# A twelve-stage decoder kernel: reordered rounded feed-forward, weight sums made a stage earlier, constant products in TensorE's waits

## What is computed

```python
def bit_linear(x, w, b):
    gamma_x = clip(max(abs(x), axis=-1, keepdims=True), 1e-05)
    x_int = clip(round(x * 127.0 / gamma_x), -128.0, 127.0)
    gamma_w = clip(mean(abs(w)), 1e-05)
    w_int = clip(round(w / gamma_w), -1.0, 1.0)
    return einsum('bsd,hd->bsh', x_int * gamma_x / 127.0, w_int * gamma_w) + b
# in the block:
h = silu(bit_linear(x, gate_w, gate_b)) * bit_linear(x, val_w, val_b)
out = bit_linear(h, out_w, out_b)
```

## Time and profile before

| | |
|---|---|
| three runs, median (lowest to highest) | 2133.7 us (2133.47 to 2135.55) |
| the profiled execution | 2131.74 us, its span 2130.0 us |
| TensorE, VectorE, ScalarE, GpSimd busy | 85%, 62%, 45%, 24% of the span |
| L0f, from the first norm instruction to that of L1a | 273.3 to 379.2 us |
| mean granted TensorE clock | 0.92 |

### The profile page before, as it was taken

How to read it: one execution, slowest core, us unless ns; L and a number is a source line. 1 busy time by engine, 2 the same in 40 slices (tenths; PEclk the granted TensorE clock), 3 DMA queues, 4 the chain that set the end, 5 groups by cost and what they waited for, 6 DMA issues and landing times. The chain is left out here.

```text
span 2130.0 us, 39122 instructions
## 1 busy us (share of the span) xinstructions
PE 1811.5 (85%) x14754; PEld 1472.3 (69%) x14758; DVE 1316.1 (62%) x2421; ACT 961.3 (45%) x1934; POOL 509.8 (24%) x557
## 2 busy tenths in 40 slices
PE   6877745689999789999757777799999998899798
PEld 4756622468999678888425665577778776788666
DVE  4575577456565654444476765788888886676632
ACT  2343445335555422222214324466667664455532
POOL 1020010023333433532030012344555552000100
PEclk9989966789999899999877987999999999999999
DMA  2020000020000101000100000000010012111000
GB/s 91 3 82 3 3 26 0 15 75 23 26 26 22 67 31 60 30 30 0 39 12 1 3 24 15 23 24 29 30 30 30 30 30 88 40 36 36 2 1 20
DMA packets 13501, 61.47 MB, mean 29 GB/s; under 512 B 1872, under 2 KB 2000, under 8 KB 11216
## 3 DMA queue, kind: packets, MB, share of 16 engines
q1 hardware_dynamic: 13392, 59.95, 8.2%
HBM read 58.90 MB, written 1.05 MB: 28 GB/s over the span
## 5 line engine op out<-in xcount | busy, mean ns | idle before, releaser
L2348 DVE SCALAR_TENSOR_TENSOR arena<-bank,arena 128x508 f32<-128x508 f32 (+2 forms) x204 | 151.7, 744 | 35.0 <-ACT arena L2344 23.0
L2473 PE MATMUL bank<-L3a_wo,L3a_y_gated 128*128 128x256 f32 x512 | 124.1, 387 | 0.0
L2679 DVE TENSOR_TENSOR L3a_decays<-L3a_decays,L3a_cb_masked 128x512 f32<-128x512 f32 x128 | 94.7, 802 | 43.8 <-ACT L3a_decays L2564 43.8
L2496 PE MATMUL bank<-L3a_xnT_high,L3a_w_high 128*128 128x512 f32 x256 | 106.4, 416 | 10.8 <-POOL L3a_w_low L2799 9.2
L2564 ACT ACTIVATE L3a_decays<-bank 128x512 f32<-128x512 f32 x128 | 66.1, 604 | 99.2 <-PE bank L2447 99.2
L1804 PE MATMUL bank<-L1f_xnT_high,L1f_high 128*128 128x512 f32 x256 | 101.6, 397 | 7.6 <-DVE L1f_hidden L1867 7.6
L2473 PEld LDWEIGHTS bank<-L3a_wo,L3a_y_gated 128*128 128x128 f32 x512 | 92.4, 190 | 17.7 <-issue 7.3
L218 PE MATMUL bank<-const,xn 128*128 128x128 f32 x192 | 47.3, 418 | 66.4 <-ACT xn L202 61.0
L1804 PE MATMUL bank<-L1f_xnT_low,L1f_high 128*128 128x512 f32 x256 | 101.2, 395 | 0.0
L1804 PE MATMUL bank<-L1f_xnT_high,L1f_low 128*128 128x512 f32 x256 | 101.0, 394 | 0.0
L1838 ACT ACTIVATE L1f_silu<-bank 128x512 f32<-128x512 f32 x64 | 38.3, 598 | 138.3 <-PE bank L1804 138.3
(11 more groups left out here) (571 smaller groups left out, 5298.8 us busy)
## 6 DMA issues: line engine op xcount, KB each, us to landing
arena<-in_L3p SPq DMA_DIRECT2D x32, 388.0 KB, 3.0
arena<-in_L1f SPq DMA_DIRECT2D x8, 1536.0 KB, 6.7
arena<-in_L1x SPq DMA_DIRECT2D x18, 384.0 KB, 3.0
arena<-in_L3x SPq DMA_DIRECT2D x18, 384.0 KB, 3.0
arena<-in_L0f SPq DMA_DIRECT2D x1, 4224.0 KB, 13.2
arena<-in_L3f SPq DMA_DIRECT2D x1, 4055.0 KB, 12.5
arena<-in_L2x SPq DMA_DIRECT2D x1, 1989.0 KB, 7.9
arena<-in_L0a SPq DMA_DIRECT2D x1, 1571.0 KB, 9.3
```

The lines of the kernel that those rows point to most:

```text
L2348: return nc.vector.scalar_tensor_tensor(dst[:, :, d:], psum[:, :, 0:P - d], wcol, dst[:, :, d:], ALU.mult, ALU.add)
L2473: mm = nc.tensor.matmul(ps[g // 2][:, (g % 2) * C:(g % 2 + 1) * C], yg[:, o, g * P:(g + 1) * P], wo[:, o, :], start=False, stop=False, ski ...
L2496: mm = nc.tensor.matmul(bank(name, half)[:, :], wm[a][:, kc, :], (xh, xl)[b][:, kc, half * HALF:(half + 1) * HALF], start=(kc + at == 0), ...
L2679: nc.vector.tensor_tensor(d, d, cbm[:, 4 * half:4 * half + 4, :].rearrange("p b t -> p (b t)"), ALU.mult).then_inc(S["dec_ready"], 1)
```

## The change

In L0f:
- The sums of absolute weights are taken in L0x, by ScalarE after its last copy: three activations with Abs and an accumulator, written to a buffer that nobody reads. The sums lie in a buffer that outlives the stage.
- The norm makes xn but no transposes and no copies. GpSimd adds the bias after x_int is ready.
- ScalarE takes the first two matrices through both steps before it rounds the third; VectorE's clip of the third comes after x_int and its copy; half of the transposed x_int is copied by ScalarE. ternary(2) comes after silu(0), and silu's table is loaded ahead.
- The loop is written out. Gates and values have separate semaphores. TensorE's order in turn n is gates(n+3), transposes of h(n), values(n+3), projection of n; three gate and three value groups stand ahead of the loop. VectorE's order is gates(n+1), addition to x of n-2, values(n+1), then the product and scales of n. ScalarE's is silu(n+1), copy of h(n-1), two roundings of h(n). g has three buffers; the scales have one column per batch.

In the norm of all other stages TensorE multiplies constants (the identity by the first columns of the constants, fp32) into bank 7: two products 512 wide at the head, and one 256 wide ahead of each wait for batches 1, 2, 3 and 5, 6, 7. In L1f six more, 512 wide, into bank 6 follow the router's products.

```diff
+    def idle(self, pe, n, width=HALF, bank=7):
+        for _ in range(n):
+            self.nc.tensor.matmul(self.k.ps[bank][:, 0:width], self.k.ident, self.k.const[:, 0:width], start=True,
+                                  stop=True)
     def tensor(self, pe):
+        self.idle(pe, 2)
         for h in range(2):
             for j in range(4):
+                if j:
+                    self.idle(pe, 1, C)
                 pe.wait_ge(self.s_xn[by_dve], (self.BY_DVE if by_dve else self.BY_ACT).index(b) + 1)
...
# l0_xattn, ScalarE
                 a.act(act)
+                act.wait_ge(k.after.s_img, 16)
+                for m in range(3):
+                    nc.scalar.activation(a.km[:, m, :, :].rearrange("p c t -> p (c t)"),
+                                         k.after.img[:, m * KC * TOK:(m + 1) * KC * TOK], ACT.Abs,
+                                         accum_out=k.wsum[:, m:m + 1])
...
# l0_ffn, TensorE
-                ln.tensor(pe)
-                pe.wait_ge(s_wsum, 3)
-                nc.tensor.matmul(ps[7][:, 0:3], k.c["ones"], wsum[:, :], start=True, stop=True).then_inc(s_tot, 1)
+                nc.tensor.matmul(ps[7][:, 0:3], k.c["ones"], k.wsum[:, :], start=True, stop=True).then_inc(s_tot, 1)
...
+                for n in range(3):
+                    gates(n)
+                    values(n)
+                for n in range(NB):
+                    s = n % 2
+                    gates(n + 3)
+                    pe.wait_ge(s_hi, n + 1)
+                    since(pe, s_hTc, n - 1)
...
+                    values(n + 3)
+                    pe.wait_ge(s_hTc, n + 1)
...
# l0_ffn, ScalarE
+                for m in range(2):
+                    rounded(m)
+                for m in range(2):
+                    ternary(m)
+                rounded(2)
+                act.wait_ge(s_xiT, 1)
+                nc.scalar.activation(xiT[:, 0, :], bank16[4], ACT.Copy).then_inc(s_xia, 1)
+                nc.scalar.preload_act_table(ACT.Silu)
+                silu(0)
+                ternary(2)
...
# l0_ffn, VectorE
-                dve.wait_ge(s_w, 16)
-                for m in range(3):
-                    nc.vector.tensor_reduce(wsum[:, m:m + 1], mats[:, m * KC * H:(m + 1) * KC * H], AX.X, ALU.add,
-                                            apply_absolute_value=True).then_inc(s_wsum, 1)
...
+                gates(0)
+                values(0)
+                for n in range(NB):
+                    gates(n + 1)
+                    if n == 2:
+                        dve.wait_ge(s_bias, 1)
+                    if n >= 2:
+                        added(n - 2)
+                    values(n + 1)
+                    dve.wait_ge(s_vread, n + 1)
+                    dve.wait_ge(s_silu, n + 1)
...
# l0_ffn, GpSimd
+                pool.wait_ge(s_xi, 1)
                 add_bias(nc, x, w["out_b"], s_bias)
# l1_ffn, TensorE
                 r.matmuls(gate_w)
+                ln.idle(pe, 6, bank=6)
                 pe.wait_ge(s_xl, 1)
```

More of the change, by code:

```diff
@@ L161, in vector @@
         between()
+        if not self.turned:
+            return
         if self.halves:
@@ L1155, in back @@
                     mm.then_inc(s_y, 1)
-                batches(pe, front, back)
             @block.scalar
@@ L1167, in _, with ternary @@
                                          scale=rgamma[:, m:m + 1]).then_inc(s_wr, 1)
-                for m in range(3):
+                def ternary(m):
                     t = slice(m * KC * H, (m + 1) * KC * H)
@@ L1185, in back, with silu @@
-                def back(act, n, s):
-                    act.wait_ge(s_hT, n)
-                    nc.scalar.activation(hiT[:, s, :], bank16[4 + s], ACT.Copy).then_inc(s_hTc, 1)
-                batches(act, front, back, back_first=True)
+                def silu(n):
+                    if n < NB:
+                        act.wait_ge(s_gread, n + 1)
+                        nc.scalar.activation(g[:, n % 3, :], g[:, n % 3, :], ACT.Silu).then_inc(s_silu, 1)
+                for m in range(2):
+                    rounded(m)
@@ new lines, in _ @@
+                for m in range(2):
[6 more added lines that the diff above has]
+                ternary(2)
+                for n in range(NB + 1):
+                    silu(n + 1)
+                    if n:
+                        act.wait_ge(s_hT, n)
+                        since(act, s_y, n - 2)
+                        nc.scalar.activation(hiT[:, (n - 1) % 2, :], bank16[4 + (n - 1) % 2],
+                                             ACT.Copy).then_inc(s_hTc, 1)
+                    if n < NB:
+                        act.wait_ge(s_scale, n + 1)
+                        since(act, s_hi, n - 1)
+                        nc.scalar.activation(hs[:, n % 2, :], g[:, n % 3, :], ACT.Identity, bias=magic[:, 0:1],
+                                             scale=hsc[:, n:n + 1]).then_inc(s_hr, 1)
+                        act.wait_ge(s_hr, n + 1)
+                        since(act, s_hT, n - 1)
+                        nc.scalar.activation(hi[:, n % 2, :], hs[:, n % 2, :], ACT.Identity,
+                                             bias=magic[:, 1:2]).then_inc(s_hi, 1)
@@ L1225, in _ @@
                 step(nc.vector.tensor_scalar(vscale[:, :], gx[:, :], gamma[:, 1:2], 1.0 / 127.0, ALU.mult, ALU.mult))
[L1226 to L1236 removed]
+                dve.wait_ge(s_xiT, 2)
@@ L1237, in front, with gates @@
+                nc.vector.tensor_copy(xiT[:, 1, :], bank16[5]).then_inc(s_xid, 1)
+                clip(2)
+                def gates(n):
+                    if n >= NB:
+                        return
+                    dve.wait_ge(s_gate, n + 1)
+                    since(dve, s_hr, n - 2)
                     for h in range(2):
                         ins = nc.vector.scalar_tensor_tensor(
-                            g[:, s, h * HALF:(h + 1) * HALF], ps[h][:, :], gscale[:, bass.ds(n, 1)],
+                            g[:, n % 3, h * HALF:(h + 1) * HALF], ps[h][:, :], gscale[:, n:n + 1],
@@ L1269, in l1_attn @@
+                for n in (NB - 2, NB - 1):
+                    added(n)
 def l1_attn(k):
```

139 lines of the change are left out of this document (52 added, 87 removed).

## The result

The changed kernel takes 2102.8 us (median of four runs, 2098.66 to 2105.61), the kernel before, run beside it, 2134.6 (four runs, 2133.47 to 2135.55): 0.985 of the time, 95% interval 0.9835 to 0.9863. That is 31.8 us less; I had predicted 2109 us, 25 less, with a range of 2101 to 2120 and 2104 to 2116 for the case that I held likeliest. The profiled execution is the fastest of the four, 2098.7 us, its span 2096.9.

The account below looks back on a forecast made before the run. In L0f's loop no engine is full and the engines wait for each other. From 2131.7 us, 23.6 less in L0f and 1.0 less from the constants give 2107.1; 2.0 added to the median makes 2109, range 2101 to 2120.

Parts of the forecast that it names:

- the case that I held likeliest: Whole kernel: the forecast's terms hold without a rival, 2104 to 2116 us, chance 0.74.
- Weight sums hidden in L0x: ScalarE's idle end of L0x: three Abs activations, 6.7 us, end 1.6 us before the next stage and cost nothing.
- Start of L0f: Head of L0f: the first gate product comes 18.8 us after the stage's start, 10.8 us earlier than before.
- Filling the pipeline: L0f, first product to first h scale: 11.6 us plus 0.7 for GpSimd; first h scale 7.4 us earlier than before.
- The loop: L0f's eight batches: VectorE sets the pace at 6.6 us a batch, 42.7 us instead of 59.5, gaining 16.8.
- the ring: Rival in L0f's loop: output comes late, a batch costs some 7.7 us, total 2117 to 2123 us; chance 0.13.
- The tail: End of L0f: the old 7.1 us plus 0.6, because ScalarE still copies h(6) when batch 7's scale is ready.
- The cost of the constants: Norms outside L0f: work behind starts later, 0.8 us in most stages, up to 2.9 in L3x, 11.6 in sum.
- Their gain: Work behind the norms starts at the full clock: 12.6 us gained together in L1a, L1x, L1f, L2x and L3a.
- the other six get nothing: L0a, L0x, L2a, L2f, L3x and L3f: the constants bring no gain that their next wait lets through.
- The rival that the norms gain: Rival in the norms: the six constants cost less, so constants give 6 to 10 us, total 2100 to 2103; chance 0.1.
- Cold constants: Rival in the norms: constants do not lift TensorE's clock, each norm gets 4.7 us, total 2159 us; chance 0.03.

Follow-up runs that it names:

- sums_in_L0f: The changed kernel with the sums of absolute weights back on VectorE in L0f, none in L0x: 2105.5 us in one run, L0f 85.45 us.
- two_ahead: The changed kernel with gates and values two batches ahead of the projection instead of three: 2123.3 us in one run, L0f 98.65 us.
- head_only: The changed kernel without the six 256-wide constants between the transposes; head pair and L1f's six stay: 2093.4 us, ratio 0.9799 to the kernel before.
- before_again: The kernel before, unchanged, profiled a second time: 2129.8 us in one run, span 2128.0 us.
- only_constants: The kernel before with all the constant products added, L0f and weight sums as before: 2129.1 us, ratio 0.9964 to the kernel before.
- no_constants: The changed kernel without any constant products, in the norms or in L1f: 2107.6 us, ratio 0.9865 to the kernel before.
- bias_early: The changed kernel with GpSimd adding the output bias once xn is read, not after x_int: 2104.2 us in one run, L0f 80.58 us.

## Why the prediction was right, and where its sizes were off

**The direction and the mechanism held**; the forecast time came out 6.2 us above the measured one. The two large errors, L0f's and the constants' gain, point the same way: both parts gave more than I priced. The 2102.8 us lie 1.8 above the lower end of the range and 1.2 below my likeliest case (2104 to 2116), and L0f's 27.5 us lie outside its own bounds, 18 to 25. The bounds had a term for waits that might be added, none for TensorE's clock rising early and none for a surcharge that was too high. Against the profiled execution, the fastest of its four, the sum of 2107.1 is 8.4 us too high: 3.9 of these lie in L0f, 4.5 in what the constants gain.

- *Weight sums hidden in L0x.* Right: 1.90 us each plus 0.19 for the accumulator (I had 2.02 and 0.2), ending 2.56 us ahead of the next stage (I had 1.6), and sums_in_L0f shows that they cost nothing there. The Trainium skill (ScalarE: Activation LUTs, Table sets: the hidden batching unit) says that abs is in every table set; the trace agrees: no load stands before Abs.
- *Start of L0f.* Right: first product after 18.45 us, predicted 18.8.
- *Filling the pipeline.* Mis-sized: from first product to first h scale 10.6 us, predicted 11.6 and 0.7 for GpSimd. I held TensorE at the lower level throughout; it rose at 292.8, 3.6 us after the first product, and VectorE waited only 0.30 for the values of batch 0 and not at all for batch 1. Clip(2) took 1.31 us instead of 1.23, a small step 0.76 instead of 0.22. So the first h scale comes 9.5 us earlier, where I said 7.4.
- *The loop.* Mis-sized: 6.25 us a batch, predicted 6.6. The 0.35 that I added for handovers was too much: in the five full batches VectorE is busy 6.08 us each and 0.17 go in short gaps between dependent steps, which together is the 6.25 that the earlier trace rows had as busy time alone. First to last scale ready takes 40.7 us instead of 42.7. The rival, the ring, is excluded: VectorE's list of waits has no entry in the loop. It is what two_ahead shows when the distance is two.
- *The tail.* Right: the last rounding of h starts 0.9 us after its scale, behind the copy of h(6); predicted 0.6. From its start to the stage's end 7.7 us, before 7.8.
- *The cost of the constants.* Right in sum, by luck to the tenth: the starts behind the norms moved by 11.5 us, predicted 11.6. The entries missed by up to 0.9 and offset each other: 0.6 to 0.8 in the plain norms (0.8), 1.6 in L1a (1.8), 2.15 in L2x (1.3), 2.5 in L3x (2.9), nothing in L1f. L0a had 1.3 where I said 0.8.
- *Their gain.* This is the other term that was too small. If every delay of a start passes on, it is 11.5 plus the 5.6 us that those eleven stages lost in sum: 17.1, predicted 12.6. L1a 1.6 (1.9), L1x 1.6 (1.45), L2x 2.1 (2.15) and L3a 2.1 (2.5) came out as said; L1f gave 6.1 instead of 4.6. Its two halves are 3.0 for the router (6.70 us in head_only, 3.71 in after; I said 2.0, since I held it bound by loading weights) and 3.0 for the six behind it (I said 2.6). L0a gave 4.3 instead of nothing. The step that is off is "the other six get nothing": for L0a I trusted the clock column where the record had not begun. The size in L0a is not firm: by before_again as the base it is 1.9, and only_constants, with the same code in L0a, took 112.3 us and gained nothing.
- *The rival that the norms gain.* The time lies in its band (2100 to 2103), and the constants' 5.6 us just short of its 6 to 10, but not by its condition: the six cost what I said. Of the 8.4 us surplus 3.9 are L0f's.
- *What I took for one thing is two.* I priced the constants as a package at minus 1. The pairs with L1f's six are worth some 14 us over no_constants (2093.4 against 2107.6), and the six between give 9 of them back. The terms for this were in my own sum: the pair costs nothing where it stands in a wait, and most of the 0.8 to 2.9 was the six's price.
- *Cold constants.* Excluded: in after, transposes and six constants together take 4.6 us in six of the norms (my 4.8), not 8.7, and the whole became faster. The granted clock over the first 4 us behind the norm is 1.00 in L1a, L1x and L2x, as I had said, and 0.81 in L3a.

How far the single profile can carry this: no_constants and after differ by 4.8 us in medians (some 3 by the ratios) and 11.4 in spans of their profiles. The sizes for L0a, L1a, L1x, L2x and L3a above lean on one profile each and carry the 1 to 3 us by which the same code differs; those for L0f and for the starts behind the plain norms repeat from kernel to kernel, as does L1f but for 300.9 in bias_early. The starts in L0a, L1a, L2x and L3x vary by 0.6 to 1.3 us among the kernels with all constants.

## What to carry to other kernels

If a loop is a ring over several engines, write down how far ahead each producer must be so that its result doesn't stand in a queue behind the consumer's answer; then the period is the busy time of the fullest engine and its short gaps, here 6.25 us. In this kernel a filler that keeps the clock up paid in a wait that existed already, ahead of TensorE's work; one placed between steps of a chain cost its length at each place, except in L1f, where the data came late anyhow. Read the level of a stretch from the durations of known instructions too, and judge an edit by the stage that repeats, not by the total.

## What was not expected of the hardware

- GpSimd's additions slow VectorE's clips of 128x2048 from 1.23 to between 1.52 and 1.63 us and a step on 128x8 from 0.17 to 0.69, while a reduction over 128x2048 keeps its 2.28; GpSimd pays too, 8.53 us, instead of 6.49 in after and 5.49 in before, where VectorE copied from PSUM and reduced beside it. The Trainium skill (GPSIMD Engine Reference, Specifications) lists the SBUF interfaces as shared with VectorE, with contention for two-port modes or two SBUF inputs. The multiplication has two inputs (2.77 instead of 2.29); that the interfaces are the cause for the clips and the small step, these runs don't show.
- The same code shows its stretches at the lower clock in other places from run to run: L0a 108.3 or 110.7 us, and nine runs of the kernel before between 2129.3 and 2138.8 us.
- The stretches at 0.50 that before shows in L0a, 30 and 90 us behind its norm (at 42.7 and 104.2), shrank or were gone with two products ahead of the norm, and were gone in before_again with none; they are back in only_constants with all of them. What moves them is open.
